# Output weights of heads 2 to 15 computed inside the first batch's heads of a latent-attention and feed-forward block, and the last join of a rounded weight chunk on GpSimd

## The reference, cut to what matters

```
x = x + attention(layernorm(x))      # 16 heads, latent queries (384) and latent keys/values (128)
x = x + ffn(layernorm(x))            # 512 -> 1536 -> 512, weights rounded to fp8 e4m3
attention:  q = rmsnorm(x @ wq_a.T) @ wq_b.T ;  kv = x @ wkv_a.T (128 + 64 rotary)
            k, v = rmsnorm(kv_c) @ wkv_b.T ;  out = softmax(q k^T * scale) v @ wo.T
ffn:        silu(gate(x) * gate_scale) * (up(x) * up_scale), then down(...) * down_scale
```

## Time and profile before

| | us |
|---|---|
| median of 3 runs | 2305.53 |
| lowest, highest | 2305.02, 2308.83 |
| the profiled execution: its time | 2308.34 |
| the profiled execution: its span | 2306.0 |
| mean granted TensorE clock | 0.994 |
| TensorE busy, share of the span | 96% |
| VectorE, ScalarE, GpSimd busy | 69%, 46%, 41% |

### The profile page before, as it was taken

How to read it: one execution, slowest core, us unless ns; L and a number is a source line. 1 busy time by engine, 2 the same in 40 slices (tenths; PEclk the granted TensorE clock), 3 DMA queues, 4 the chain that set the end, 5 groups by cost and what they waited for, 6 DMA issues and landing times.

```text
span 2306.0 us, 36511 instructions
## 1 busy us (share of the span) xinstructions
PE 2222.7 (96%) x10952; PEld 1027.7 (45%) x10952; DVE 1590.2 (69%) x3334; ACT 1062.1 (46%) x2335; POOL 956.2 (41%) x657
## 2 busy tenths in 40 slices
PE   6899989999999999999999999999999999999988
PEld 5334444445444454444544445444454445444443
DVE  7688877877558774677647776477655877567762
ACT  4466564444344543445425453354533454345532
POOL 1336335363344523455334543446324363343322
PEclk9999999999999999999999999999999999999999
DMA  6265633554144531545206451164513554144420
GB/s 249 64 147 131 128 85 85 121 111 97 24 116 105 121 66 28 138 103 121 56 20 153 103 119 46 38 146 103 116 28 79 121 112 96 23 99 107 102 62 18
DMA packets 698513, 218.37 MB, mean 95 GB/s; under 512 B 680208, under 2 KB 680464, under 8 KB 697360
## 3 DMA queue, kind: packets, MB, share of 16 engines
q1 hardware_dynamic: 698384, 216.77, 41.2%
HBM read 40.78 MB, written 8.39 MB: 21 GB/s over the span
## 4 chain that ended last, share of the span: by engine, by line
PE 73%; DVE 14%; ACT 4%; issue 4%; DMA 2%; SPq 2%; POOL 0%; DVEq 0%; ACTq 0%; POOLq 0%
PE bank L762 11%; PE bank L272 8%; PE bank L274 8%; PE bank L273 8%; PE scores L772 6%; PE bank L621 4%; PE bank L623 4%; PE bank L622 4%; PE scores L610 4%; PE scores L274 4%; PE scores L273 4%; PE scores L272 4%; DVE arena L1254 3%; DMA arena<-arena 2%; PE scores L607 2%
## 5 line engine op out<-in xcount | busy, mean ns | idle before, releaser
L1436 POOL TENSOR_TENSOR arena<-arena 128x1024 f16<-128x1024 f32 x256 | 545.0, 2129 | 709.3 <-ACT arena L926 709.3
L924 ACT ACTIVATE arena<-scores,shift 128x512 f32<-128x512 f32 x512 | 357.3, 698 | 600.4 <-DVE shift L1234 589.0
L1254 DVE SCALAR_TENSOR_TENSOR arena<-bank,rden,arena 128x512 f32<-128x512 f32 x512 | 350.7, 744 | 149.5 <-PE bank L274 149.5
L1232 DVE TENSOR_REDUCE mx<-scores 128x1 f32<-128x512 f32 x512 | 353.0, 689 | 10.1 <-PE scores L274 4.9
L926 ACT ACTIVATE arena<-scores,shift 128x512 f16<-128x512 f32 x512 | 358.5, 700 | 0.0
L762 PE MATMUL bank<-arena,WFF 128*128 128x512 f16 x1408 | 319.5, 381 | 12.9 <-DVE arena L1319 11.0
L1474 POOL TENSOR_TENSOR arena<-arena 128x512 f16<-128x512 f32 x96 | 114.8, 1196 | 323.3 <-ACT arena L980 323.3
L1038 DVE SCALAR_TENSOR_TENSOR arena<-bank,arena 128x512 f16<-128x512 f32 (+2 forms) x269 | 179.6, 669 | 58.6 <-ACT arena L917 53.9
L762 PEld LDWEIGHTS bank<-arena,WFF 128*128 128x128 f16 x1408 | 137.5, 98 | 181.2 <-DVE arena L1319 14.8
L272 PE MATMUL bank<-WVO,arena 128*128 (+1 forms) x512 | 194.1, 379 | 10.1 <-DVE arena L1038 10.1
L610 PE MATMUL scores<-arena 128*128 128x512 f16 x512 | 195.4, 382 | 0.0
(11 more groups left out here) (164 smaller groups left out, 3477.5 us busy)
## 6 DMA issues: line engine op xcount, KB each, us to landing
arena<-arena SPq DMA_TRANSPOSE x706, 2.7
arena<-w_ffn SPq DMA_DIRECT2D x24, 384.0 KB, 3.4
arena<-x SPq DMA_DIRECT2D x8, 1024.0 KB, 5.4
out<-arena SPq DMA_DIRECT2D x32, 256.0 KB, 2.3
arena<-x SPq DMA_DIRECT2D x14, 512.0 KB, 3.9
WFF<-w_o SPq DMA_DIRECT2D x4, 1024.0 KB, 18.6
arena<-w_nope SPq DMA_DIRECT2D x4, 768.0 KB, 14.0
arena<-down_scale SPq DMA_DIRECT2D x8, 256.0 KB, 3.3
```

The costliest lines, as they stand in the source:

```text
L924: act.activation(P32[:, t, :], SC[:, t, :], ACT.Exp, scale=EXP_SCALE, bias=shift[:, t:t + 1], accum_out=esum[:, par, t:t + 1]).then_inc(s[ ...
L1232: dve.tensor_reduce(mx[:, t:t + 1], SC[:, t, :], AX_X, ALU.max).then_inc(s["mxr"], 1)
L1254: dve.scalar_tensor_tensor(out=XR[:, t, :], in0=OBANK[t][:, :], scalar=rden[:, t:t + 1], in1=XR[:, t, :], op0=ALU.mult, op1=ALU.add).then_ ...
L1436: pool.tensor_tensor(PL[:, par, two, :], P32[:, two, :], PH[:, par, two, :], ALU.subtract).then_inc(s["pl"], 1)
```

## The change

It touches four things.

1. **Where the output weights are made.** W(0) and W(1) are still made in setup, after the four first rotated blocks and the first absorbed queries (`N_VO_SETUP = 2`). W(h) for h = 2 to 15 is made in batch 0: TensorE issues `output_weights(h)` ahead of scores of head h (h = 15: ahead of the last scores), ScalarE `output_hi(h)` ahead of the exponentials, VectorE `output_lo(h)` between the sums and the context split. All but W(0) pass through bank BT, the bank of the second tile of `project_out`, so `output_weights(h)` waits for `outr >= 4(h-2)+2`, the second `add_out` of head h-2.
2. **Where the fp32 sources lie.** g_o is loaded into WVO itself, so each W(h) replaces its own w_o(h) in place; the layout of WVO becomes [head, hi/lo, column]. The four DMAs of w_o lose their wait. g_v moves from XR's memory to WFF, g_pe to memory of PT. The XR load moves up to stand right behind w_o on SP's queue, without its wait.
3. **Chunk plan.** Chunks 0 to 14 go with heads 0 to 14; chunk 15 with feed-forward tile 0, none with tile 1, chunks 16 to 23 with tiles 2 to 9. In the feed-forward the join of a chunk stands ahead of the next tile's work instead of behind it.
4. **The last join instruction** (sum into WFF) moves from VectorE (L1066) to GpSimd, in heads behind the low halves of the probabilities and ahead of the next norm, in the feed-forward ahead of the tile's L1474.

TensorE's heads 2 to 13 of batch 0 are written out in place of the loop. A new wait stands ahead of the rotated blocks of the setup: all twelve absorbed weights split. The diff, cut to its core (the parts follow the file: names, SyncE, TensorE, VectorE, GpSimd; ScalarE's program changes in the same order as VectorE's):

```
-NC_HEADS = NH - 2
+NC_HEADS = NH - 1
+N_VO_SETUP = 2
 def chunks_of(i):
-    return [i - 1] if 1 <= i <= NC_HEADS else []
+    return [i] if i < NC_HEADS else []
+def ffn_chunk(c):
+    if c == 0:
+        return NC_HEADS
+    return NC_HEADS + c - 1 if 2 <= c <= NC_FF - NC_HEADS else None
...
-        WVO = sb("WVO", [P, 2, NH, H], F16)
+        WVO = sb("WVO", [P, NH, 2, H], F16)
...
-        g_o = wff32[:, 0:NH * H].rearrange("p (h n) -> p h n", h=NH)
+        g_o = WVO.rearrange("p h a n -> p (h a n)").bitcast(F32).rearrange("p (h n) -> p h n", h=NH)
...
         def vo_step(h):
-            return (BC, BO)[h % 2][:, :], lambda p: WVO[:, p, h, :], ncol[:, NQ:NQ + 1]
+            return (BC if h == 0 else BT)[:, :], lambda p: WVO[:, h, p, :], ncol[:, NQ:NQ + 1]
...
             for q in range(4):
-                sp.wait_ge(s["w_lo"], N_A if (q + 1) * 4 * H <= o_pe else N_A + N_PE)
                 sp.dma_start(g_o[:, 4 * q:4 * q + 4], w_o[:, 4 * q:4 * q + 4]).then_inc(ld_o[q], 16)
+            sp.dma_start(XR, x[0].rearrange("(t p) d -> p t d", p=P)).then_inc(s["ld_res"], 16)
...
-            sp.wait_ge(s["w_psum"], N_AB + N_VO)
-            sp.dma_start(XR, x[0].rearrange("(t p) d -> p t d", p=P)).then_inc(s["ld_res"], 16)
...
             def output_weights(h):
-                if h == 0:
+                if h == 1:
                     pe.wait_ge(s["kb"], 1)
-                elif h == 1:
-                    pe.wait_ge(s["ktl"], 1)
-                else:
-                    pe.wait_ge(s["w_lo"], N_A + N_PE + N_AB + h - 1)
+                elif h > 1:
+                    pe.wait_ge(s["outr"], (h - 2) * NT + 2)
...
             def setup_keys_and_rotated():
                 key_transposes()
-                done = 0
-                for n in range(N_ROT_FFN):
-                    if n >= NT:
-                        pe.wait_ge(s["rot4"], n - NT + 1)
-                    rotated(0, n, SC[:, n % NT])
-                    while done < NH * (n + 1) // N_ROT_FFN:
-                        output_weights(done)
-                        done += 1
-                    if n == NT - 1:
-                        absorb(0, 0)
+                pe.wait_ge(s["w_lo"], N_A + N_PE + N_AB)
+                for n in range(NT):
+                    rotated(0, n, SC[:, n])
+                absorb(0, 0)
+                for h in range(N_VO_SETUP):
+                    output_weights(h)
                 absorb(1, 1)
+                pe.wait_ge(s["ktl"], 1)
+                rotated(0, NT, RBANK[0])
...
             def head_step(b, pair, par, first=False, ahead=True, weights=False):
+                if weights:
+                    output_weights(pair * 2 + par)
                 scores(b, pair, par)
...
             def join_chunk(c):
...
                 dve.tensor_tensor(f_clip, f_b16[k], f_clip, ALU.subtract).then_inc(s["f_diff"], 1)
-                dve.wait_ge(s["f_diff"], c + 1)
-                dve.wait_ge(s["f_aw"], c + 1)
-                w = WFF[:, c * FC:(c + 1) * FC]
-                dve.tensor_tensor(w, w, f_clip, ALU.add).then_inc(s["f_free"], 1)
...
             def setup_rotated():
+                for n in range(NT):
+                    rot_products(0, n, SC[:, n, :])
                     if n >= 1:
                         rot_lo(0, n - 1)
                 qa_lo(0, 0)
+                output_lo(0)
+                rot_lo(0, NT - 1)
+                output_lo(1)
                 qa_lo(1, 1)
+                rot_products(0, NT, RBANK[0])
+                rot_lo(0, NT)
...
                 sums_of_head(g - 1, 1 - par)
+                if weights:
+                    output_lo(i)
...
                 maxima(base)
+                if first:
+                    for c in chunks_of(0):
+                        round_chunk(c)
                 qa_lo(base + 2, 0)
                 rot_products(b, N_ROT_FFN + 1, RBANK[(N_ROT_FFN + 1) % 2])
                 rot_lo(b, N_ROT_FFN)
+                if first:
+                    for c in chunks_of(0):
+                        join_chunk(c)
...
                 for c in range(NF):
+                    if first and c >= 1 and ffn_chunk(c - 1):
+                        join_chunk(ffn_chunk(c - 1))
                     tile_step(c)
...
+            def join_chunk(c):
+                pool.wait_ge(s["f_diff"], c + 1)
+                pool.wait_ge(s["f_aw"], c + 1)
+                w = WFF[:, c * FC:(c + 1) * FC]
+                pool.tensor_tensor(w, w, f_clip, ALU.add).then_inc(s["f_free"], 1)
```

More of the change, by code:

```diff
@@ L665, in before, with head_step @@
                 return (pair, 0) if par else (pair - 1, 1)
-            def head_step(b, pair, par, first=False, ahead=True):
+            def head_step(b, pair, par, first=False, ahead=True, weights=False):
+                if weights:
+                    output_weights(pair * 2 + par)
                 scores(b, pair, par)
@@ L690, in attention @@
                 head_step(b, 0, 1)
-                with pe.Fori(1, NH // 2 - 1) as pair:
-                    head_step(b, pair, 0)
-                    head_step(b, pair, 1)
+                if first:
+                    for i in range(2, NH - 2):
+                        head_step(b, i // 2, i % 2, weights=True)
+                else:
+                    with pe.Fori(1, NH // 2 - 1) as pair:
+                        head_step(b, pair, 0)
+                        head_step(b, pair, 1)
                 final = NH // 2 - 1
+                if first:
+                    output_weights(NH - 2)
                 scores(b, final, 0)
@@ L962, in attention @@
                     i = NH - 2 + k
-                    head_step(i, base, k, ahead=False, chunks=chunks_of(i) if first else ())
+                    head_step(i, base, k, ahead=False, chunks=chunks_of(i) if first else (), weights=first)
                     if not last:
@@ L1290, in attention @@
                     part = i - start if 0 <= i - start < 4 and not last else None
-                    head_step(i, b, i % 2, ahead=i < NH - 2, chunks=chunks_of(i) if first else (), part=part)
+                    head_step(i, b, i % 2, ahead=i < NH - 2, chunks=chunks_of(i) if first else (), part=part,
+                              weights=first)
             def last_of_attention(b):
@@ L1462, in attention, with ffn @@
                             rotate(b, n)
+                    if first:
+                        for c in chunks_of(i):
+                            join_chunk(c)
                     if 0 <= i - start < NT and not last:
                         next_norm(b, i - start, stg)
-            def ffn(b, last):
+            def ffn(b, last, first):
                 if not last:
@@ L1484, in batch @@
                 attention(b, last, first)
-                ffn(b, last)
+                ffn(b, last, first)
             pool.wait_ge(s["ld_k"], 32)
```

64 lines of the change are left out of this document (31 added, 33 removed).

## The result

The changed kernel takes 2283.0 us (median; 2282.1 to 2284.9), the kernel before 2305.3 us (2304.6 to 2308.8): ratio 0.990, 95% interval 0.989 to 0.991. The profiled execution took 2283.28 us, its span is 2280.4 us.

The account below looks back on a forecast made before the run. TensorE, busy 96% of the span, was taken as the bound, with VectorE's loop pacing most batch 0 heads. Terms -16.5 (setup through head 0), +7.0 (heads), -3.9 (feed-forward) sum to -13.4 us: 2292 us, range 2285 to 2300.

Parts of the forecast that it names:

- The first scores: Setup: fourteen output weights leave, 13.4 us of TensorE's time; first scores at 68.8 us, 20.2 earlier.
- The heads: Batch 0: twelve steps take 148.4 us against 143.3, +5.1; output weights 14 and 15 add 1.9, in all +7.0.
- TensorE's own head: Batch 0: TensorE's work per head grows from 11.22 us by an output weight's 0.96, to 12.15.
- The feed-forward: Batch 0: 5.6 us stall shrinks to 3.4, 2.0 booked; last chunk's 1.9 us wait vanishes with GpSimd's add; sum -3.9.
- The change touches setup and batch 0: Starting step: only stretches in setup and batch 0 where TensorE waits or runs at the lower clock can give time back.
- The rival that gave 2285.5: Feed-forward stall and head 0's lag both close, the half-clock stretch goes too: -20 us; chance 0.10.
- Head 0: Batch 0: VectorE enters late, maxima of head 1 lose 3.7 us; net 16.5 us earlier at `add_out`, bounds 15 and 18.
- The join: Last join instruction on GpSimd: 1.6 us by length, up to 2.1 if it first waits for VectorE.
- The rival that named the port: GpSimd's join takes SBUF's port ahead of VectorE, whose loop grows 1.6 to 2.1 us per head: 2311 us; chance 0.08.
- The "0.50" per head for L1066: Batch 0 heads: VectorE's loop loses L1066 with its wait, 0.50 us a step, and gains `output_lo`, about 0.66.
- Hidden share: Batch 0 heads: of the moved weights' 13.4 us, 6.4 are hidden in stalls of VectorE's making.

Follow-up runs that it names:

- e1: Kernel before, with TensorE's heads 2 to 13 of the first batch written out in place of the loop; 2296.6 us.
- e2: Kernel before, with 70 increments of a semaphore nobody waits for put ahead of everything on TensorE; 2299.9 us.
- e5: Changed kernel with all sixteen output weights made in setup and none in the heads; 2293.5 us.
- e9: Changed kernel with 212 semaphore increments ahead of everything on TensorE; 2304.2 us.
- e4: Changed kernel with the last join of a rounded chunk back on VectorE; 2295.1 us.
- e8: Changed kernel with, in head 1, VectorE's rot_lo ahead of the join of chunk 1 and ScalarE's query-product conversion ahead of its rounding of chunk 1; 2280.6 us.
- e10: e4 with GpSimd's norm in heads 7 to 10 of the first batch waiting until VectorE has joined the head's chunk; 2291.5 us.
- e7: Changed kernel with VectorE's rot_lo in head 1 put ahead of the join of chunk 1; 2280.1 us.
- e6: Changed kernel with the old chunk plan: 14 chunks in the heads, ten in the first ten feed-forward tiles; 2286.0 us.
- e12: e8 with 40 semaphore increments ahead of TensorE's first wait; 2283.6 us.
- e3: Changed kernel with 186 semaphore increments ahead of everything on TensorE; 2301.4 us.

## Why the prediction was right and wrong

**What held.** The first scores: 68.8 forecast, 67.9 measured. The kernel before has some 1.5 us more in this stretch in its profiled execution than e1 and e2, which have the same setup (87.35 and 87.68), so the true gain is nearer 19.5 than 21.2, which is also e5's 19.25. The heads: +5.1 forecast over twelve steps, +5.9 measured, and +7.0 both times over all of them (18.4 - 15.2 + 3.8); TensorE's own head 12.15 against 12.08. That the sum fits so well is partly luck: the step from head 0 to head 1 took 2.3 us more than its forecast, the other steps that VectorE sets took 1.0 less together, and TensorE's seven 0.5 less. The feed-forward: -3.9 against -3.79, stall 3.4 against 3.7 with 1.0 more in a second one. At the start of batch 1 the forecast was -13.4 and the traces say -15.2, or some -13.7 without that 1.5.

**What failed** is the step ahead of all others: "The change touches setup and batch 0", and with it a sum that ends at batch 1. It books nothing for batches 1 to 7. Their mean length fell from 276.43 to 274.74, which is 10.1 us over six batches in the profiled executions; by the medians, from which the profiled execution of before lies 3 us away, 22.3 less the 13.7 to 15.2 of batch 1's start leaves 7 to 9 us. That is the miss. By stage the 10.1 us are 5.9 in the step from head 3 to head 4, 2.5 in the feed-forward and 1.7 in the step from head 1 to head 2. e1 shows that the place of TensorE's code alone gives 7.0 of them, the 5.9 included, and e9 ties this step to the fetch that falls on its transposes. The other 3.1 do not look like TensorE's code: e4, whose TensorE program is that of the changed kernel, gives 3.4 back with the join on VectorE. By what mechanism stays open. The rival that gave 2285.5 came near the number for a wrong reason: neither the half-clock stretch nor the lag closed. Sixteen matmuls still took 5.18 us instead of 3.62 behind the stall, the first 2.2 us of them at a granted clock of 0.50.

**Head 0.** With the measured 21.2 us at the first scores, maxima of head 1 would keep pace at 101.54 - 21.2 = 80.4; they start at 84.20, a lag of 3.8 us where 3.7 was forecast. The net is 18.4 where 16.5 was forecast, 0.4 above its upper bound; with the 1.5 us above it is 16.9, within the bounds.

**The join.** Its duration was bounded well, 1.6 to 2.1 us: the 24 took 1.63 to 2.02, mean 1.78. L1063 did win against it in every head but it was not the only instruction exposed: in head 1 the two `rot_lo` came behind it. The rival that named the port was right about the mechanism in that one head (1.4 us) and wrong about the place. The "0.50" per head for L1066 was mis-sized: in e4 the steps that VectorE sets are 0.6 longer each, and those of heads 8 to 11 1.26. In all e4 says 7.2 us over the heads and 2.1 in the feed-forward. The term left out that GpSimd's norm in heads 7 to 10 collides with the join's instructions; I had booked it only as a delay to transposes. The Trainium skill, "SBUF — State Buffer", section "Who interferes with whom", has GpSimd or VectorE hold a shared pair of ports for a whole instruction. Three experiments agree with it: 1.28 and 2.73 us for L1210 in e8 and the changed kernel, 0.56 and 1.40 for L1078 in e10 and e4, and e7's 1.44 us.

**The feed-forward** came out right in its sum. Its split into two parts did not: I tied the first to the plan (no chunk on ScalarE at tile 1) and the second to the join on GpSimd, as if they added up. Alone they give 1.7 (e4) and 0.2 (e6), together 3.8.

**Hidden share.** I forecast that the weights' 13.4 us of TensorE's time would cost 7.0 in the heads, 6.4 hidden; the 7.0 already counts the join taken off VectorE. Against e5, which has that too, the heads pay 9.1, so by the same measure 4.3 are hidden. What hiding is worth is still 10.1 us, since in setup the fourteen cost 19.25 with the waits for their banks, not 13.4.

**Open.** Which fetch makes the step from head 1 to head 2 take 11.5 to 12.8 us in most versions and 11.2 to 11.4 in e2 and e12 isn't settled. In the latter two the fetch at 3.2 or 7.0 us comes at 1.7 to 2.4, but batch 1 of the kernel before has one at 3.2 and a step of 11.22. No version was made that has both this step and the feed-forward short; with e8's batches of 274.8 us, 0.7 us each is left there. One thing in the traces bears on it. In all fourteen kernels the step takes 11.2 to 11.5 us in batches 1 and 7, and there q14 has no packet in the first 11 us. In batches 2 to 6 it has one: at 2.5 to 3.1 us in before, e1, e4 and e10, where the step's mean is 12.3 to 12.6; at 1.2 to 2.2 in the changed kernel and the versions of it other than e4, e10 and e12, where it is 11.7 to 12.0; at 0.2 to 2.0 in e2 and e12. No run moved q14's packets alone, so this is a correlation.

## What to carry to other kernels

Write out or add instructions anywhere on an engine, and every loop behind it may change its time: before booking "unchanged code, no change", look at where the instruction packets fall among the transfers that the loop waits for, and allow for it, here from 1.2 us less (e1) to 0.5 us more (e9) in a batch of 275; compare versions stage by stage, so that this term doesn't hide or fake the gain of an edit. When an instruction moves from VectorE to GpSimd, list what both queues hold in the 2 us behind it, each head apart: here the same move shielded four heads from a collision and made one in a fifth. Put first what the next stage waits for, and weight work, which has slack, behind it.

## What the runs showed of the hardware

- An instruction fetch of TensorE is one packet of 16384 bytes of 0.9 to 2.0 us. Beside a pair of probability transposes it lengthened the issue from 2.65 to 3.71 us (L358) or from 3.72 to 4.84 us (L357), and the landing from 2.8 to 4.2 us. I had not counted with it, and by the medians the batches behind the change gave about a third of its gain.
- At the turn of a batch TensorE stood 0.8 to 1.5 us ahead of a batch's first scores, with nothing that the profile shows to release it, in e2 and e12 and in no other version. That a fetch held it up is inferred.
- A semaphore increment at TensorE's start took 0.158 us, with nothing else to do (186 of them in e3, 212 in e9).
